# A macaron block on one core: the first expert layer cut into two units of 4 and 12 row tiles, and the first attention batch prepared between the second unit's slots

## What is computed

```python
x = x + 0.5 * ffn(layernorm(x))       # 8 experts, the best one for each row
x = x + attention(layernorm(x))       # 16 heads of 8 channels, causal, within a batch
x = x + 0.5 * ffn(layernorm(x))
# ffn: scores = x @ Wg.T; prob = softmax(scores); e = argmax(prob)
#      y = (gelu(x @ W1[e].T + b1[e]) @ W2[e].T + b2[e]) * prob[e]
# attention: L = q k^T / sqrt(8); Ly = q ky^T / sqrt(8)
#      agg = sum(exp(clip(Ly)) * mask); r = log|L| - log(agg)
#      w = softplus(r) * mask; out = (w / sum(w)) v; out @ w_proj.T
```

## Time and profile before

| | us |
|---|---|
| median of 3 runs | 466.5 (465.37 to 467.26) |
| profiled execution, its own time | 465.7 |
| its span, first to last instruction | 463.9 |
| first slot matmul of layer 1 to first score matmul | 36.1 to 119.7 |
| first score matmul to first slot matmul of layer 2 | 119.7 to 396.7 |

### The profile page before, as it was taken

How to read it: one execution, slowest core, us unless ns; L and a number is a source line. 1 busy time by engine, 2 the same in 40 slices (tenths; PEclk the granted TensorE clock), 3 DMA queues, 4 the chain that set the end, 5 groups by cost and what they waited for, 6 DMA issues and landing times.

```text
span 463.9 us, 7907 instructions
## 1 busy us (share of the span) xinstructions
PE 330.0 (71%) x2362; PEld 201.8 (44%) x2362; DVE 306.6 (66%) x634; ACT 285.9 (62%) x830; POOL 172.6 (37%) x258
## 2 busy tenths in 40 slices
PE   2817999916677545677968597778879671799991
PEld 1706999803233111212323233234343561689990
DVE  6681222146689979979899999999996748122210
ACT  1204444503789998979899989997775320344550
POOL 6357777411143570014110250106300205777741
PEclk9999999967589655767787779799898655699997
DMA  8716685234563069903000030003001351668530
GB/s 270 212 52 212 199 205 169 76 103 126 154 173 92 0 167 230 231 8 92 2 1 1 1 92 0 3 1 92 1 2 56 104 203 36 210 197 191 159 90 0
DMA packets 38626, 48.85 MB, mean 105 GB/s; under 512 B 4581, under 2 KB 27119, under 8 KB 38332
## 3 DMA queue, kind: packets, MB, share of 16 engines
q1 hardware_dynamic: 33756, 37.67, 29.6%
q0 software_dynamic: 3680, 8.59, 7.1%
q10 hardware_dynamic: 1152, 2.11, 1.4%
HBM read 24.82 MB, written 7.22 MB: 69 GB/s over the span
## 4 chain that ended last, share of the span: by engine, by line
PE 41%; DVE 19%; ACT 15%; issue 9%; DMA 6%; POOL 5%; SPq 4%; POOLq 0%; DVEq 0%
PE PS L1245 11%; PE PS L1229 10%; ACT R L763 6%; DVE R L1054 5%; PE PS L1360 4%; SPq L433 4%; ACT R L771 4%; DMA R<-QPS 3%; ACT CL L763 3%; PE PS L1165 2%; DVE R L1039 2%; PE PS L1342 2%; DVE CL L1039 2%; PE PS L1385 2%; PE PS L1286 2%
## 5 line engine op out<-in xcount | busy, mean ns | idle before, releaser
L1054 DVE TENSOR_TENSOR R<-PS,MB 128x1024 int32<-128x1024 int32 (+1 forms) x96 | 97.8, 1034 | 13.8 <-PE PS L1342 11.3
L679 ACT ACTIVATE R<-PS,R 128x128 f32<-128x128 f32 x184 | 52.4, 368 | 59.1 <-PE PS L1229 59.1
L771 ACT ACTIVATE R<-R 128x1024 f32<-128x1024 f32 x64 | 80.2, 1262 | 10.6 <-DVE R L1054 10.5
L763 ACT ACTIVATE R<-R 128x384 f32<-128x384 f32 (+2 forms) x192 | 77.1, 408 | 8.4 <-DVE R L1039 8.4
L1327 PE MATMUL PS<-R 64*128 64x512 bf16 (+3 forms) x256 | 40.3, 371 | 32.8 <-DVE CL L1039 14.8
L1039 DVE SCALAR_TENSOR_TENSOR R<-PS,MA 128x1024 f32<-128x1024 f32 x64 | 59.6, 947 | 1.3 <-PE PS L1327 0.7
L1360 PE MATMUL PS<-R,V 128*32 128x256 f32 (+3 forms) x512 | 57.0, 534 | 4.6 <-ACT R L771 4.5
L958 DVE SCALAR_TENSOR_TENSOR R<-PS,scoef,R 128x128 f32<-128x128 f32 x46 | 15.9, 350 | 61.6 <-PE PS L1245 61.6
L1229 PE MATMUL PS<-R 128*128 128x128 f32 x368 | 53.1, 291 | 4.1 <-DVE R L949 4.1
L1245 PE MATMUL PS<-R 128*128 x368 | 53.5, 289 | 0.0
L526 POOL DMA_INDIRECT R<-rows_d,R x46 | 44.3, 964 | 22.1 <-issue 18.1
(11 more groups left out here) (164 smaller groups left out, 473.9 us busy)
## 6 DMA issues: line engine op xcount, KB each, us to landing
R<-w SPq DMA_DIRECT2D x38, 258.0 KB
R<-R SPq DMA_DIRECT2D x48, 128.0 KB, 2.4
R<-w SPq DMA_DIRECT2D x2, 2048.0 KB, 10.1
QPS<-R SPq DMA_DIRECT2D x32, 128.0 KB, 2.4
R<-R SPq DMA_DIRECT2D x16, 256.0 KB, 6.5
R<-w ACTq DMA_DIRECT2D x8, 258.0 KB
rows_d<-X SPq DMA_DIRECT2D x8, 256.0 KB, 7.5
rows_d<-R SPq DMA_DIRECT2D x8, 256.0 KB, 3.7
```

The source lines that it names most:

```text
L679: last = act.activation(HT[:, k % 2, c * P:(c + 1) * P], PS[:, k % 2, c * P:(c + 1) * P], ACT.Gelu, bias=W1[:, k, F + c:F + c + 1])
L763: act.activation(e, e, ACT.Exp, scale=SCALE, accum_out=aggf[:, ds(s + (2 * i + par) * STEPS, 1)])\
L771: act.activation(w, w, ACT.Ln, bias=1.0, scale=1.0).then_inc(s_ln, 1)
L1054: dve.tensor_tensor(weights(v)[:, :, at:at + n].bitcast(i32), PS[:, SLOTS[slot(b_fill(v, g))], 0:n].bitcast(i32), spread(mask, 1, 2), ALU. ...
```

## The change

Layer 1 works on two units, tiles 0 to 3 and 4 to 15, each with its own routing, its own slots (4 + 7 = 11 and 12 + 7 = 19, so 30 in place of 23), its own store of rows in DRAM, and its own count of scatters. The first unit's slots run while the second unit is normalised and routed. Batch 0 of X is read back when the first unit's 11 scatters have landed, between slots 17 and 18 on VectorE, and normalised, transposed, projected and stacked between slots 18 and 28. Batches 1 to 3 are read back after the last slot; their moments and normalisation move into `after(0)`, `after(1)` and `after(2)` of VectorE's attention loop, and projections 3 to 11 come two steps later than before. For these parts the reciprocal deviation is a chain of 12 instructions on VectorE in place of the square root on ACT. SP's order of stacks becomes 0, 1 (between the last loads of W1), 2 to 6, scaled q 0, 8, 7. `finish(r, s)` is `slot_out` and, where one is due, `copy_xt`. Layer 2 is one unit, with the order of before; its loops are written out. Buffers and PSUM banks change to fit. The core of the diff:

```diff
-ROUTE_TILES = (((0, 8), (8, 16)), ((0, 12), (12, 16)))
-POOL_ROWS = (12, 8)
+UNITS = ((0, 0, 4), (0, 4, 16), (1, 0, 16))
+PARTS = ((0, 0, 4), (1, 4, 16), (2, 0, 12), (2, 12, 16))
+VECTOR_ROWS = (0, 4, 8)
+ROWS_AT = {3: (2,), 5: (3, 4), 6: (5,), 7: (6,), 8: (7,)}
...
 SP
+            for b in range(NB):
+                sp.wait_ge(s_x[b], 16)
+                store_x(min(b, 1), b)
+            store_xn(0, 0, 0)
...
+            for b in range(1, NB):
+                store_xn(1, 0, b)
-            for i in range(6):
-                stack(i)
+            for n in range(RING, SLOTS_IN[0]):
+                load_w1(0, n)
+                if n == 19:
+                    sp.wait_ge(s_xd[0], 16 * unit_slots(0))
+                    reload_x(0)
+                if n == 27:
+                    stack(0)
+                if n == 28:
+                    stack(1)
+            sp.wait_ge(s_xd[1], 16 * unit_slots(1))
+            for b in range(1, NB):
+                reload_x(b)
+            for i in range(2, 7):
+                stack(i)
             scaled_q_stack(0)
-            for i in (8, 7, 6):
-                stack(i)
+            stack(8)
+            stack(7)
...
 POOL
+            slots_known(0)
+            for n in range(11):
+                gather(0, n)
+            for n in range(3):
+                scatter(0, n)
+            slots_known(1)
+            for n in range(11, 19):
+                gather(0, n)
+            for n in range(3, 11):
+                scatter(0, n)
+            for n in range(19, 27):
+                gather(0, n)
+            for n in range(11, 14):
+                scatter(0, n)
+            for n in range(27, SLOTS_IN[0]):
+                gather(0, n)
+            for n in range(14, SLOTS_IN[0]):
+                scatter(0, n)
...
 ACT
+            deviations(0)
+            copy_xnt(0, 0)
+            exp_scores(0)
+            first_weights(0)
+            copy_xnt(0, 1)
+            for n in range(SLOTS_IN[0]):
+                gelu(0, n)
+                if n < 2:
+                    copy_xnt(0, n + 2)
+                if n == 4:
+                    exp_scores(1)
+                if n == 20:
+                    copy_xnt(1, 0)
...
 VectorE
+                if part not in ACT_PARTS:
+                    link(dve.tensor_scalar(var, mv[:, b0 * TB:b1 * TB, 1], LN_EPS, None, ALU.add))
...
+                    for _ in range(3):
+                        link(dve.scalar_tensor_tensor(out=tmp, in0=inv, scalar=-0.5, in1=inv,
+                                                      op0=ALU.mult, op1=ALU.mult))
+                        link(dve.tensor_tensor(tmp, tmp, var, ALU.mult))
+                        link(dve.scalar_tensor_tensor(out=inv, in0=tmp, scalar=1.5, in1=inv,
+                                                      op0=ALU.add, op1=ALU.mult))
...
+            dve.wait_ge(s_x[0], 16)
+            moments(0)
+            layer_norm(0)
+            dve.wait_ge(s_x[1], 16)
+            moments(1)
+            bias_terms()
+            route_scores(0)
+            dve.wait_ge(s_x[2], 16)
+            moments(2)
+            route_ranks(0)
+            slot_starts(0)
+            slot_hots(0)
+            row_hots(0)
+            slot_experts(0)
+            dve.wait_ge(s_x[3], 16)
+            moments(3)
+            slot_tokens(0)
+            deviation(1)
+            normal_rows(0, 1)
+            copy_first(0, 0)
+            normal_rows(0, 2)
+            copy_first(0, 1)
+            coefficient_hots(0)
+            normal_rows(0, 3)
+            copy_first(0, 2)
+            slot_coefficients(0)
+            copy_first(0, 3)
+            finish(0, 0)
+            finish(0, 1)
+            route_scores(1)
+            finish(0, 2)
+            finish(0, 3)
+            route_ranks(1)
+            finish(0, 4)
+            slot_starts(1)
+            slot_hots(1)
+            row_hots(1)
+            finish(0, 5)
+            slot_experts(1)
+            finish(0, 6)
+            slot_tokens(1)
+            coefficient_hots(1)
+            finish(0, 7)
+            finish(0, 8)
+            slot_coefficients(1)
+            plain_mask()
+            finish(0, 9)
+            for n in range(10, 18):
+                finish(0, n)
+            reloaded(0)
+            finish(0, 18)
+            layer_norm(2)
+            for n in (19, 20):
+                finish(0, n)
...
 VectorE, after(s)
+                if s == 0:
+                    reloaded(1)
+                    layer_norm(3)
+                if s == 1:
+                    reloaded(2)
+                    reloaded(3)
+                    deviation(4)
+                if s == 2:
+                    normal_rows(1, 2)
+                    normal_rows(1, 3)
+                if FIRST_PROJECTIONS <= s < len(PROJECTIONS):
+                    remainder(s)
...
 TensorE
+            turn(0, 0)
+            gate(0, 0, 4)
+            ranks(0)
+            slot_tokens(0)
+            turn(0, 1)
+            for n in range(SLOTS_IN[0] + 1):
+                if n < 4:
+                    first_transpose(0, n)
+                if n == first_slot(1):
+                    down(0, n - 1)
+                    slot_transposes(0, group_of(0, n))
+                if n < SLOTS_IN[0]:
+                    up(0, n)
+                if n == 1:
+                    slot_coefficients(0)
+                if n >= 1 and n != first_slot(1):
+                    down(0, n - 1)
+                if n < 2:
+                    pe.wait_ge(s_xnt, n + 2)
+                    turn(0, n + 2)
+                if n == 2:
+                    pe.wait_ge(s_scf, 1)
+                    gate(1, 4, 16)
+                if n == 3:
+                    ranks(1)
+                if n == 6:
+                    slot_tokens(1)
+                if n == 7:
+                    slot_coefficients(1)
+                if n == 20:
+                    turn(1, 0)
+                if n == 21:
+                    pe.wait_ge(s_wa, 16)
+                    project(0)
+                if n == 22:
+                    project(1)
+                if n == 23:
+                    q_v_rows(0)
+                if n == 24:
+                    q_v_rows(1)
+                if n == 25:
+                    project(2)
+            pe.wait_ge(s_h, SLOTS_IN[0])
+            pe.wait_ge(s_y, SLOTS_IN[0])
```

More of the change, by code:

```diff
@@ L20 @@
 from contextlib import ExitStack
+from dataclasses import dataclass
 P = 128
@@ L467, in _ @@
             sp.wait_ge(s_xr, NB)
-            store_x(NB - 1)
-            store_xn(2, NB - 1)
-            slots(1)
-            sp.wait_ge(s_out, 16 * NS)
+            store_x(2, NB - 1)
+            store_xn(2, 2, NB - 1)
+            for n in range(RING, SLOTS_IN[1]):
+                load_w1(1, n)
+            sp.wait_ge(s_out, 16 * SLOTS_IN[1])
         @block.gpsimd
@@ L672, in gelu @@
-            def gelu(r, s, k):
-                act.wait_ge(s_up, s + (r * NS + 1))
-                for c in range(FC):
-                    if c == 0 and (not isinstance(s, int) or s >= 2):
-                        act.wait_ge(s_dn, s + (r * NS - 1))
-                    last = act.activation(HT[:, k % 2, c * P:(c + 1) * P],
-                                          PS[:, k % 2, c * P:(c + 1) * P], ACT.Gelu,
-                                          bias=W1[:, k, F + c:F + c + 1])
-                last.then_inc(s_h, 1)
@@ L1141, in _ @@
                 if s == LN_EARLY:
-                    layer_norm(4, XN1)
-            layer_norm(5, XN1)
-            route(1, 0)
-            ffn(1)
+                    layer_norm(5)
+            layer_norm(6)
+            route_scores(2)
+            route_ranks(2)
+            route_scores(3)
+            route_ranks(3)
+            slot_starts(2)
+            slot_hots(2)
+            row_hots(2)
+            slot_experts(2)
+            slot_tokens(2)
+            coefficient_hots(2)
+            for n in range(4):
+                copy_first(1, n)
+                if n == 1:
+                    slot_coefficients(2)
@@ L1460, in _ @@
                     pe.wait_ge(s_aot, STEPS // 2)
[L1461 to L1467 removed]
+                    for b in range(NB - 1):
+                        if b >= 2:
+                            pe.wait_ge(s_xnt, 2 * NB + b - 1)
+                        turn(2, b)
+            gate(2, 0, 12)
+            pe.wait_ge(s_xnt, 2 * NB + 2)
+            turn(2, NB - 1)
+            gate(3, 12, 16)
+            ranks(2)
+            ranks(3)
+            slot_tokens(2)
+            for n in range(SLOTS_IN[1] + 1):
+                if n < 4:
+                    first_transpose(1, n)
+                if n < SLOTS_IN[1]:
+                    up(1, n)
+                if n == 1:
+                    slot_coefficients(2)
+                if n >= 1:
+                    down(1, n - 1)
 def kernel(L0_attn_x, L0_attn_w_qkv, L0_attn_w_ky, L0_attn_w_proj, L0_ffn_Wg, L0_ffn_W1, L0_ffn_b1,
```

863 lines of the change are left out of this document (470 added, 393 removed).

## The result

The changed kernel takes 493.2 us (median of 4 runs, 492.3 to 495.5) beside 466.6 us of the kernel before: 1.058 of its time, interval 1.0545 to 1.0617. I had forecast 479 us, in a range of 461 to 489. The sign was right; the loss is twice the forecast one.

What follows compares the result with a forecast made beforehand. No engine bounds the whole: PE sets layer 1's slots, nobody the stretch after them, ACT and VectorE attention steps 3 to 11. Terms +5.8 + 10.6 - 3.2 = +13.2 on 465.7 us gave 479 us, range 461 to 489.

Steps and rivals of the forecast that it cites:

- First slot: Start of layer 1's slots: first `up` at 26.9 us instead of 36.1, -9.2 us.
- Slots 0 to 10: First unit's slots: PE and VectorE wait for each other during unit 1's routing, +16.2 us, 10.3 of it waits.
- Seven more slots: Slots 11 to 29 at 2.23 us each on PE, +15.6 us; gathers of slots 19 to 22 cost zero, at worst 2.
- Batch 0 between the slots: Between slots 20 and 25: PE's transposes, projections and rows plus a 1.4 us wait for VectorE, +7.2 us.
- SP's stacks ahead of W1: Last slots: W1 loads 28 and 29 queue behind stack DMAs on SP, +1.7 us, bounds 0 and 5.
- The gap: Between last slot's output and first attention scores: 26.2 us shrink to 0.5, -25.7 us.
- Steps 0 to 11: Attention: moved VectorE work and later projections cost +10.6 us, +8.7 in steps 0 to 2 and +1.9 in 3 to 11.
- Step 16: Attention: PE no longer waits there for stack 6, -3.2 us, from 0 to 4.6.
- Layer 2 at 0: Second layer: keeps its order, so its time changes by 0.
- B: First unit's slots: 5 of the first 11 run at half PE clock, +10 us, 489 us; chance 0.12.
- C: Slots: SP's sixteen DMAs or POOL's gathers of slots 19 to 22 hold PE, 484 us; chance 0.10.

Runs made afterwards that it cites:

- a_warm: Changed kernel with unread extra matmuls filling PE's idle time ahead of its two waits for the second unit's routing: 489.5 us, ratio 1.052 to the kernel before.
- a_later_gath: Changed kernel with unit 1's slot tokens and coefficients on PE later, and POOL's gathers of slots 11 to 22 ahead of its scatters: 486.5 us, 1.045.
- a_best_r: Later-series rerun of the changed kernel with five order edits (routing products, gathers, last W1 loads, query_part, v_rows): 473.4 us, ratio 1.016 to the kernel before.
- a_later: Changed kernel with unit 1's slot tokens one slot later and slot coefficients two slots later on PE: 490.8 us, ratio 1.054 to the kernel before.
- a_w1act: Changed kernel with the last two W1 loads issued from ScalarE's queue instead of SP's: 486.7 us, ratio 1.046 to the kernel before.
- a_serial_r: Later-series rerun of the changed kernel with batch 0's normalisation, transposes, projections, rows and stacks behind the last slot: 500.3 us, ratio 1.075 to the kernel before.
- b_late: Kernel before with only projections 3 to 11 and the q and v rows moved to the change's later steps: 470.1 us, ratio 1.011.
- a_pool: Changed kernel with POOL's query_part at place 12 of the step's emission instead of 4: 487.4 us, ratio 1.051 to the kernel before.
- a_vrows: Changed kernel with VectorE's copy of v's rows one group earlier in its step: 487.6 us, ratio 1.050 to the kernel before.
- b_stack6: Kernel before with only SP's stack order from the change, stack 6 ahead of the scaled q: 462.1 us, ratio 0.992.
- b_best: Kernel before with stack 6 ahead of the scaled q and POOL's query_part at place 12 instead of 9: ratio 0.990 in its first, slowed series.

## Why the forecast was wrong

The sign and most of the terms stood. By the forecast's own steps:

1. **First slot: right.** -9.2 forecast, 26.18 for 36.13 us is -9.95.
2. **Slots 0 to 10: mechanism right, half clock left out.** From slot 0 to up(11) 50.6 us, so +21.9 and not +16.2. The two waits were forecast to within a microsecond (2.04 and 3.81). Most of the 5.7 more are products at half clock, about 1 us for each group of eight: six such groups stand between slot 0 and up(11) in the changed kernel, three of them behind the two waits, and two in the slots from which I took my 28.7. I priced them as a rival, with a chance of 0.12, but pauses were in my own sum, so the half clock behind them belonged in it. a_warm shows 3.7 to 4.1 of the 5.7; the rest was not followed.
The Trainium skill's page "TensorE: Matmul & The Clock Gate" (section on HAM oscillation) says that bursts with pauses between them start again at half rate; the changed kernel's trace agrees, with 2.06 us for 1.06 behind each of the three waits over 2 us, and a_warm with 1.14 when the pause is filled. It does not hold row by row: behind a_later_gath's wait of 2.52 us and a_best_r's of 2.95 the first eight products take 1.13 us and only the next are slower (1.94 and 1.59), and the groups at 32.72 and 44.14 are slow without such a wait.
3. **Seven more slots: right.** The rows of slots 19 to 22 held nobody up in the changed kernel, with PE 5 us behind the forecast at up(11) and POOL's first gather for the second unit at 62.05 us. a_later shows the margin as it was worked out: the rows land at 87.6 (forecast 87.4), and PE, 4.4 us ahead of the forecast there, waits 4.36 us. So this term cost nothing, but whatever makes PE faster before it is lost to it, until POOL's order changes.
4. **Batch 0 between the slots: right.** 1.95 us of wait for 1.4, and some 1.5 at half clock behind it, which I had not counted; a_warm has 1.86 us of wait there and none.
5. **SP's stacks ahead of W1: mis-sized.** 3.12 us of wait and about 1.5 at half clock, where I took 1.7; inside the bounds of 0 and 5. Undone in a_w1act, it gives 4.7 at the first scores. With 3 and 4, up(11) to the first scores took 57.0 us for 53.7 forecast.
6. **The gap: right**; a_serial_r shows 22.3 us for one batch's chain when it stands alone. In sum the first scores were 14.1 us late for 5.8 forecast, of which -0.8 in 1, +5.7 in 2, +3.3 in 3 to 5.
7. **Steps 0 to 11: the step that failed.** +10.6 forecast, +19.0 measured. Its first half stood: steps 0 to 2 took 21.6 us for 23. Its second half, "these nine steps had 0.5 us of free ACT time, so +1.9", was +11.7. I had counted what ACT has to do and not when each result is wanted. Even that count was short: ACT is busy 5.1 us more in these steps, where 1.9 and the free 0.5 make 2.4; two copies of transposed rows, 0.57 us each, were among what it lacked. b_late, which has nothing but the later projections, shows +8.1 in these steps: q and v rows wait on PE for a copy on VectorE that comes an `after(s)` later, clips wait for scores behind them, and the last terms meet POOL's `query_part` at steps 9 to 11 (a_pool, a_vrows). Some 2 of these 8.1 are the clock in the interval from step 3 to 4, and the changed kernel's trace has that and 1.5 more from step 7 to 8; whether the new order brings this about or one execution's chance is open. The other 3.6 were not followed singly.
8. **Step 16: right.** -3.2 forecast, -3.7 measured; b_stack6 alone gives -3.3 between the first clips of step 12 and step 16 (174.7 to 198.2 us for 174.3 to 201.1).

Layer 2 at 0 stood: at step 16 the changed kernel is 29.4 us behind, at the end 29.8. Of the rivals, B and C were both partly true, beside the forecast and not in place of it: I had treated as alternatives what adds up. My reading is that this is also why the range ended too low.

## What to carry to other kernels

Price a moved piece of work by the instruction that waits for it and what is queued behind that on its engine, not by the busy share of the stage it moves to; here a shift by two steps with no work added cost 8 us in the later steps and gave back 3.5 in the first ones. Where a sum has pauses of TensorE, give what the products behind them may cost at the lower clock a term with bounds (here from nothing to 3 us for one pause), and add small queue risks instead of making them rivals. Test each part of a large change alone on the old kernel: one part of this one, seven stacks instead of six before the scaled q, was worth 0.8%, and with one move on POOL, which is not part of the change, 1.8%, while the whole costs 5.8%.

## What the runs showed of the hardware that I had not expected

PE's clock level does not follow from the length of the pause alone. The pause of 1.47 us in the attention had four slow instructions behind it in the changed kernel (1.88 us) and four fast ones in b_late (1.10). The eight products behind a wait for W1 took 2.05 us after 3.12 us in the changed kernel, and 1.13 after 2.95 in a_best_r. The same interval from step 3 to 4 took 4.3 us in six kernels and 6.3 to 6.5 in three (the changed one, a_serial_r and a_best_r), at clocks of 1.00 and 0.56 in the two windows shown, and that from step 7 to 8 took 3.9 us in five of these nine and 5.4 to 6.0 in the other four: a single trace carries some 2 us of the clock's choice at each. And one series of runs held every kernel up for 45 to 50 us, in b_best's trace as two stops of 20.5 us with PE and ACT idle and VectorE nearly so, while POOL went on gathering; ratios to the kernel run beside it stayed usable, absolute times did not. Its cause was not found, and a later series under the same chip number did not show it.
